# Attention in a fused transformer layer: a fifth place for k and q, loads issued in the projections' program, and value products in five places of a step

## The chip, the core and the metric

The kernel runs on one core of one Trainium2 chip. The metric is the device time of one execution in microseconds (us); less is better. The engines of a core are named as in the profile: PE is TensorE's matmul and PEld its weight load, DVE is VectorE, ACT ScalarE, POOL GpSimd and SP SyncE, which here only issues DMAs. A change of under 0.5% is taken as no change.

## The reference

One layer: attention with a window, and a mixture of experts behind it. Cut to what matters here:

```
x: (8, 512, 256)                      # 8 batches, 512 tokens, 16 heads of 16
h = layernorm(x)
Q, K, V = h @ Wq + bq, h @ Wk + bk, h @ Wv + bv
scores = Q K^T / 4 + mask             # mask: |i - j| <= 64, or i == 0, or j == 0
x = x + softmax(scores) V @ Wo + bo
x = x + experts(layernorm(x)) + shared(layernorm(x))
```

The change touches the projections Q, K, V and the attention; the output projection and the experts are as they were.

## The kernel before

**Three programs in a row.** `project`, `attend` and `mlp` each open a block of their own: every engine has its list of instructions in the block, and all engines meet at a barrier between two blocks. SP reaches the barrier behind `project` only when it has seen all its stores of q and k land (`out_s`, L217 and L218).

**The projections** go over the 8 batches. PE makes q and k of a batch, ACT and DVE split them into high and low parts in the tile `qk`, POOL copies one column (L241), and SP stores the batch's parts to the DRAM tensor `qk_parts` (L209): one DMA of 2064 KB a batch. At the start POOL clears `qs` and `ks` with three memsets (L225, L227, L229), one behind the other.

**The attention** goes over 32 steps `u`; a step is four heads of one batch (`b = u // 4`, `t = u % 4`). Its q and k lie in place `t` of `qs` and `ks`, in 96 rows: six DMAs of 129 KB bring them from `qk_parts` (`load`, L492). Each step does this:

- PE makes 16 score products into `ps_s`, a ring of three buffers (L625). DVE takes the maximum of each with the mask (L548), and then three small operations turn the 16 maxima into the tile `mt`; SP copies `mt` into two more rows of `qs` (`m_rows`, L500, four DMAs).
- PE makes the exponents in eight jobs of two products each (L643, L646; in the first two jobs also the mask, L637), into two buffers of `ps_p`. ACT takes the exponential of each (L601), and POOL clears what lies outside the window (L467).
- PE multiplies with the values: `times_v(u, i)` for four tiles `i` of keys (L673 and L679 for tile 0; L653, L657, L658 and L683 for the others). ACT takes the result out of `ps_o` (L579) and SP stores it (L504).

**The order is written out by hand.** PE runs the scores two steps ahead: in job `n` of step `u` come two scores of step `u + 2`, then the exponents of step `u`, and behind jobs 5 and 7 the value products of step `u - 1` (L691 to L699). SP issues in step `u` the maxima's rows of step `u + 1`, then, once the exponents of step `u - 1` are all made, the load of step `u + 3` into the place that step left, then the store of step `u - 2` (L521 to L528). Every fourth step DVE also takes the reciprocals of the softmax sums (L564) and SP moves them.

Names of semaphores that the text uses: `z_s` (a batch of q and k is ready to store), `qk_in` (a step's loads have landed), `mx_s` (a maximum is taken, its score buffer is free), `st_s` (a job's exponents are made), `exp_s`, `sel_s` and `nrm_s` (ACT's exponential, POOL's selection, ACT's copy out of `ps_o`).

Of the kernel before, what the change touches and what calls it, by code (L numbers as in the profile page):

```python
# [29 lines left out]
P = 128  # L30
# [16 lines left out]
HQ = 4  # L47
# [4 lines left out]
RING = 3  # L52
ZC = P + 1
# [30 lines left out]
def build(nc, d):  # L84

    with ExitStack() as ctx:
        def sem(name):
            return ctx.enter_context(nc.semaphore(name))

        def scratch(name, shape):  # L90
            return nc.dram_tensor(name, shape, F32).ap()

        d["qk"] = scratch("qk_parts", (B, 4, UB, DH, HQ, ZS))
        d["ot"] = scratch("attn_t", (B, UB, P, S))
        d["rden"] = scratch("rden", (B, NH, S))
# [16 lines left out]
        project(nc, d, sem, tally, ident, bias, eps, ks, qs, v, mask, ident16)  # L112
        attend(nc, d, sem, tally, ks, qs, v, mask, ident16)
        att.close()
        mlp(nc, d, sem, tally, ident, eps)
# [27 lines left out]
def project(nc, d, sem, tally, ident, bias, eps, ks, qs, vs, mask, ident16):  # L143
    with ExitStack() as ctx:
# [44 lines left out]
        with nc.Block() as block:  # L189
            @block.sync  # L190
            def _(sp):
# [210 lines left out]
def attend(nc, d, sem, tally, ks, qs, vs, mask, ident16):  # L402
    with ExitStack() as ctx:
# [15 lines left out]
        qk_in = [sem(f"a_qk_in{s}") for s in range(UB)]  # L419
        ones_s = sem("a_ones")  # L420
        v_s = sem("a_v")
        m_in = [sem(f"a_m_in{s}") for s in range(UB)]
# [35 lines left out]
        with nc.Block() as block:  # L458
# [28 lines left out]
            def _(sp):  # L487
                def load(u):
                    b, t = u // UB, u % UB
                    for dst, parts in ((qs, (0, 0, 1)), (ks, (2, 3, 2))):  # L490
                        for n, part in enumerate(parts):
                            sp.dma_start(dst[n * DH:(n + 1) * DH, t].bitcast(F32), d["qk"][b, part, t]).then_inc(qk_in[t], 16)  # L492

                def m_rows(u):

                    t = u % UB
# [43 lines left out]
            def _(dve):  # L540
                def maxima(u):
# [15 lines left out]
                    if u >= 2:  # L557
                        dve.wait_ge(m_in[(u - 2) % UB], ((u - 2) // UB + 1) * 16 * MROWS)
# [14 lines left out]
            def _(act):  # L573
# [7 lines left out]
                def far_rows(u):  # L581

                    t = u % UB
                    act.wait_ge(m_in[t], (u // UB + 1) * 16 * MROWS)
# [25 lines left out]
            def _(pe):  # L610
                def score(u, g):

                    b, t = u // UB, u % UB
                    j, h = SCORES[g]
                    n = u * SG + g
                    if g == 0:
                        pe.wait_ge(qk_in[t], (b + 1) * 16 * LOADS)
# [9 lines left out]
                def exponents(u, n):  # L627

                    b, t = u // UB, u % UB
# [29 lines left out]

                def times_v(u, i):  # L660

                    s = u % 2
# [7 lines left out]
                    for h in range(HQ):  # L670
                        rows, v = slice(32 * h, 32 * h + 32), vx[:, s, i, h * VW:(h + 1) * VW]
                        if i == 0:
                            pe.matmul(ps_o[rows, 0:N0], v, pt[0][:, s, h, 0:N0], start=True, stop=True, skip_group_check=True)  # L673
                        else:
                            near(rows, v, pt[i][:, s, h], i)
                    for h in range(HQ):
                        rows, v = slice(32 * h, 32 * h + 32), vx[:, s, i, h * VW:(h + 1) * VW]
                        if i == 0:
                            last = pe.matmul(ps_o[rows, N0:S], v[0:1], pt[0][0:1, s, h, N0:S], start=False, stop=True,  # L679
                                             skip_group_check=True)  # L680
                        else:
                            z = FAR[i]
                            last = pe.matmul(ps_o[rows, 0:1], v, pt[i][:, s, h, z:z + 1], start=False, stop=True,  # L683
                                             skip_group_check=True)
                    if i == NT - 1:
                        last.then_inc(av_s, 1)

# [3 lines left out]
                for u in range(NU):  # L691
                    for n in range(SJ):
# [1296 lines left out]
```

## Time and profile before

| | us |
|---|---|
| median of 3 runs | 1362.97 |
| lowest and highest | 1359.61, 1365.81 |
| the profiled execution | 1356.66 |
| its span, first to last instruction | 1354.9 |

The profiled execution is 6.3 us under the median. In its span, the projections take the first 110 us, the attention lies between 110 and 491 us, and the rest is the output projection and the experts. Times in rows are from the start of the span. A row of the timeline has the start, the duration (of a merged row from its first start to its last end), the engine, the line, the operation, what is written and read, the count, and in brackets how long the engine sat idle before it and what ended that. SPq rows are issues of DMAs, not their transfers.

### The profile page before, as it was taken

The numbers are of one execution on the slowest core, as the hardware profiler recorded it, in microseconds if no ns is written. First come the engines' busy times: TensorE is split into PE (matmuls) and PEld (weight loads), VectorE is DVE, ScalarE is ACT, GpSimd is POOL, SyncE is SP. The second block draws the span as 40 slices with busy tenths as digits, with TensorE's granted clock in tenths as the row PEclk, the third lists the DMA queues.
The fourth block names the chain that finished last, engine by engine and source line by source line (L and its number), as shares of the span: only waits on it lengthen the run. The fifth ranks groups of instructions, "written<-read, shape, count | busy, mean of one in ns | idle before, by whom it ended". The sixth has DMA issues, their size and how long they took to land. (4 is left out here: it accounts for less than half of the span.)

```text
span 1354.9 us, 23514 instructions
## 1 busy us (share of the span) xinstructions
PE 1191.9 (88%) x8906; PEld 979.6 (72%) x8906; DVE 868.0 (64%) x2246; ACT 599.0 (44%) x959; POOL 612.8 (45%) x698
## 2 busy tenths in 40 slices
PE   2995898989899833899999599999999999999997
PEld 1883665656666523798887488888888888888886
DVE  7885676766666405674788686666666666666641
ACT  1440555555555522444322255555455555454542
POOL 6000333434343324452200157667676676776654
PEclk9995899999998876789999799999999999999999
DMA  2778367566656245531012344444434444444411
GB/s 87 248 267 157 58 105 109 87 108 98 112 91 105 51 129 152 162 114 51 32 40 101 109 140 125 109 112 123 124 103 116 125 125 125 107 105 116 125 31 16
DMA packets 62094, 149.09 MB, mean 110 GB/s; under 512 B 14736, under 2 KB 31520, under 8 KB 52640
## 3 DMA queue, kind: packets, MB, share of 16 engines
q1 hardware_dynamic: 49328, 128.72, 36.3%
q0 software_dynamic: 12656, 18.90, 7.7%
q8 instruction: 69, 1.13, 0.4%
q14 instruction: 41, 0.34, 0.1%
HBM read 104.73 MB, written 42.34 MB: 109 GB/s over the span
## 5 line engine op out<-in xcount | busy, mean ns | idle before, releaser
L548 DVE CUSTOM_DVE_ANT_0 junk_s<-ps_s,mask 128x258 bf16<-128x258 f32 (+2 forms) x512 | 211.9, 472 | 123.5 <-PE ps_s L625 122.1
L601 ACT ACTIVATE pt<-ps_p 128x516 f32<-128x516 f32 (+2 forms) x256 | 167.7, 682 | 158.3 <-PE ps_p L643 94.5
L467 POOL TENSOR_SCALAR_AFFINE_SELECT pt<-pt 128x256 f32<-128x256 f32 x352 | 132.3, 415 | 230.3 <-ACT pt L601 230.3
L1775 POOL TENSOR_TENSOR h_lo<-h,h_hi 128x512 fp32r<-128x512 f32 x128 | 178.8, 1408 | 119.6 <-ACT h_hi L1811 119.3
L1885 PE MATMUL ps_gu<-xt_hi,w_hi 128*128 128x512 f32 x512 | 202.9, 396 | 2.1 <-DVE xt_lo L1834 2.1
L625 PE MATMUL ps_s<-ks,qs 96*128 96x258 f32 (+2 forms) x512 | 164.6, 380 | 45.6 <-DMA ks<-qk_parts 43.6
L1885 PE MATMUL ps_gu<-xt_lo,w_hi 128*128 128x512 f32 x512 | 200.1, 391 | 0.0
L1885 PE MATMUL ps_gu<-xt_hi,w_lo 128*128 128x512 f32 x512 | 199.9, 390 | 0.0
L1850 DVE TENSOR_TENSOR h<-ge,ps_gu 128x512 f32<-128x512 f32 x128 | 87.8, 686 | 168.2 <-ACT ge L1805 147.7
L1712 DVE TENSOR_TENSOR w_lo<-w,w_hi 128x768 fp32r<-128x768 f32 x128 | 174.1, 1364 | 31.3 <-ACT w_hi L1707 27.8
L1784 POOL DMA_INDIRECT out<-ys,idx x64 | 137.1, 2142 | 72.3 <-ACT ys L1821 57.4
L625 PEld LDWEIGHTS ps_s<-ks,qs 96*128 96x128 f32 x512 | 99.3, 207 | 87.1 <-DMA ks<-qk_parts 45.2
L1902 PE MATMUL ps_y<-w_hi,h_hi 128*128 128x256 f32 x512 | 146.4, 286 | 3.4 <-ACT ys L1821 3.4
L1902 PE MATMUL ps_y<-w_lo,h_hi 128*128 128x256 f32 x512 | 144.8, 283 | 0.0
L1902 PE MATMUL ps_y<-w_hi,h_lo 128*128 128x256 f32 x512 | 144.8, 283 | 0.0
L1805 ACT ACTIVATE ge<-ps_gu 128x512 f32<-128x512 f32 x128 | 76.2, 596 | 120.9 <-PE ps_gu L1885 120.2
L1679 POOL DMA_INDIRECT xg<-h_rows,idx x64 | 62.8, 981 | 125.4 <-DVE idx L1670 105.6
L1707 ACT ACTIVATE w_hi<-w 128x768 fp32r<-128x768 f32 x128 | 106.4, 837 | 16.9 <-PEq L852 16.9
L1885 PEld LDWEIGHTS ps_gu<-xt_hi,w_hi 128*128 128x128 f32 x512 | 96.6, 189 | 21.3 <-issue 2.5
L1885 PEld LDWEIGHTS ps_gu<-xt_hi,w_lo 128*128 128x128 f32 x512 | 96.4, 188 | 20.5
L1885 PEld LDWEIGHTS ps_gu<-xt_lo,w_hi 128*128 128x128 f32 x512 | 96.7, 189 | 18.5
L1902 PEld LDWEIGHTS ps_y<-w_hi,h_hi 128*128 128x128 f32 x512 | 98.0, 191 | 7.2 <-ACT ys L1821 6.6
(220 smaller groups left out, 2399.8 us busy)
## 6 DMA issues: line engine op xcount, KB each, us to landing
w<-in_We SPq DMA_DIRECT2D x48, 1024.0 KB, 4.9
qk_parts<-qk SPq DMA_DIRECT2D x8, 2064.0 KB, 7.7
qs<-qk_parts SPq DMA_DIRECT2D x96, 129.0 KB, 3.8
ks<-qk_parts SPq DMA_DIRECT2D x96, 129.0 KB, 5.6
x<-in_x SPq DMA_DIRECT2D x16, 512.0 KB, 8.6
attn_t<-on SPq DMA_DIRECT2D x32, 256.0 KB, 5.6
ot<-attn_t SPq DMA_DIRECT2D x32, 128.0 KB
rd<-rden SPq DMA_DIRECT2D x16, 256.0 KB
```

Of the source, the lines that this page charges most:

```text
L467: last = pool.affine_select(out=part, in_=part, pattern=[[0, HQ], [sign, WIN]], compare_op=ALU.is_ge, fill=0.0, base=sign * (n % 2) * WIN, ...
L548: dve.tensor_tensor_reduce(junk[:, (u * SG + g) % RING, 0:n], ps_s[:, (u * SG + g) % RING, 0:n], m, 1.0, -3e38, ALU.add, ALU.max, mx[:, u ...
L601: act.activation(dst, src, ACT.Exp, scale=SCALE).then_inc(exp_s, 1)
L625: pe.matmul(out, q, k, start=True, stop=True).then_inc(sc_s, 1)
L1707: act.activation(self.hi[:, s, cs], self.w32[:, cs], ACT.Copy).then_inc(self.hi_s, 1)
L1712: eng.tensor_tensor(self.lo[:, s, cs], self.w32[:, cs], self.hi[:, s, cs].bitcast(F32), ALU.subtract).then_inc(self.lo_s, 1)
L1775: pool.tensor_tensor(h_lo[:, m], h32[:, (e * KI + m) % HB], h_hi[:, m].bitcast(F32), ALU.subtract).then_inc(hlo_s, 1)
L1784: pool.indirect_dma_start(d["out"], bass.IndirectOffsetOnAxis(ap=idx[:, e % SLOTS, c:c + 1], axis=0), ys[:, e % 2, c], None, compute_op=AL ...
L1805: act.activation(ge[:, m % 2], ps_gu[:, m % 2, 0], ACT.Gelu).then_inc(gelu_s, 1)
L1850: dve.tensor_tensor(h32[:, (e * KI + m) % HB], ge[:, m % 2], ps_gu[:, m % 2, 1], ALU.mult).then_inc(h_s, 1)
L1885: last = pe.matmul(ps_gu[:, m % 2, n], l, r, start=c == 0, stop=c == 3 * KD - 1)
L1902: last = pe.matmul(ps_y[:, t % 2, 0:D], l, r, start=c == 0, stop=c == 3 * KI - 1)
```

## The change

It does five things. `qs` and `ks` get five places for steps instead of four (`SL`), and their semaphores too. The loads of the first five steps are issued in the projections' program, behind the store of the sixth batch and ahead of those of the last two; before, those of the first four steps were issued at the start of the attention's program. In the attention's steps, the load of step `u + 4` stands where that of step `u + 3` stood. The value products stand behind jobs 2, 4, 5 and 6 instead of in two groups behind jobs 5 and 7. And the far part of tile 0 is split off as `far_v`, behind job 3.

```
+SL = 5
...
-        ks = att.enter_context(nc.sbuf_tensor("ks", [P, UB, HQ, ZS], F32R))
-        qs = att.enter_context(nc.sbuf_tensor("qs", [P, UB, HQ, ZS], F32R))
+        ks = att.enter_context(nc.sbuf_tensor("ks", [P, SL, HQ, ZS], F32R))
+        qs = att.enter_context(nc.sbuf_tensor("qs", [P, SL, HQ, ZS], F32R))
...
+        qk_in = [sem(f"a_qk_in{s}") for s in range(SL)]
...
                 with sp.Fori(0, B // 2 - 1) as i:
                     step(i, 0, True)
                     step(i, 1, True)
+                sp.wait_ge(ready, 4)
+                for u in range(SL):
+                    sp.wait_ge(out_s[u // UB % 2], (u // UB // 2 + 1) * 16)
+                    load_step(sp, d, ks, qs, qk_in, u)
                 step(B // 2 - 1, 0, False)
                 step(B // 2 - 1, 1, False)
...
+def load_step(sp, d, ks, qs, qk_in, u):
+
+    for dst, parts in ((qs, (0, 0, 1)), (ks, (2, 3, 2))):
+        for n, part in enumerate(parts):
+            sp.dma_start(dst[n * DH:(n + 1) * DH, u % SL].bitcast(F32), d["qk"][u // UB, part, u % UB]).then_inc(qk_in[u % SL], 16)
...
-                for u in range(UB):
-                    load(u)
                 m_rows(0)
...
-                    if 1 <= u <= NU - UB:
+                    if 1 <= u <= NU - SL:
                         sp.wait_ge(st_s, u * SJ)
-                        load(u + UB - 1)
+                        load_step(sp, d, ks, qs, qk_in, u + SL - 1)
...
+                def far_v(u):
+
+                    for h in range(HQ):
+                        rows, v, p = parts_of(u, 0, h)
+                        pe.matmul(ps_o[rows, N0:S], v[0:1], p[0:1, N0:S], start=False, stop=True, skip_group_check=True)
...
-                        if u >= 1 and n in (5, 7):
-                            times_v(u - 1, n - 5)
-                            times_v(u - 1, n - 4)
-                for i in range(NT):
+                        if u >= 1 and n == 2:
+                            times_v(u - 1, 0)
+                        if u >= 1 and n == 3:
+                            far_v(u - 1)
+                        if u >= 1 and 4 <= n <= 6:
+                            times_v(u - 1, n - 3)
+                times_v(NU - 1, 0)
+                far_v(NU - 1)
+                for i in range(1, NT):
                     times_v(NU - 1, i)
```

SP's list between the two programs, before: the last two stores of q and k, the barrier, and then the loads of four steps.

```order
L212 COMPARE_AND_BRANCH
L209 DMA qk_parts<-qk 128x8x516 [waits p_z] x2
L189 UNCONDITIONAL_BRANCH [waits p_out1,p_out0]
L486 UNCONDITIONAL_BRANCH [waits barrier_Pool_Activation_PE_DVE_SP_release]
L492 DMA qs<-qk_parts 16x2064 x3
L492 DMA ks<-qk_parts 16x2064 x3
```

The same place now, from the end of the loop over batches (three of the four waiting pairs on `p_out0` left out):

```order
L214 COMPARE_AND_BRANCH
L412 DMA qs<-qk_parts 16x2064 [waits p_out0,p_ready]
L412 DMA qs<-qk_parts 16x2064 x2
L412 DMA ks<-qk_parts 16x2064 x3
...
L412 DMA qs<-qk_parts 16x2064 [waits p_out1]
L412 DMA qs<-qk_parts 16x2064 x2
L412 DMA ks<-qk_parts 16x2064 x3
L211 DMA qk_parts<-qk 128x8x516 [waits p_z] x2
L191 UNCONDITIONAL_BRANCH [waits p_out1,p_out0]
L498 UNCONDITIONAL_BRANCH [waits barrier_Pool_Activation_PE_DVE_SP_release]
L506 DMA qs<-mt 2x16x32 [waits a_mt]
```

The 30 loads now stand ahead of two stores for which the barrier waits, and the maxima's rows come first in the attention's program.

PE's list in the second half of a step before (`ps_s` scores, `ps_p` exponents, `ps_o` value products), from job 4:

```order
L625 MATMUL ps_s<-ks,qs 128x258 [waits a_mx] x2
L646 MATMUL ps_p<-qs,ks 128x258 [waits a_exp]
L646 MATMUL ps_p<-qs,ks 128x258
L673 MATMUL ps_o<-pt,vx 32x192 [waits a_nrm,a_v,a_exp]
L673 MATMUL ps_o<-pt,vx 32x192 x3
L679 MATMUL ps_o<-pt,vx 32x320 x4
L653 MATMUL ps_o<-pt,vx 32x256 [waits a_sel]
L653 MATMUL ps_o<-pt,vx 32x256 x3
L683 MATMUL ps_o<-pt,vx 32x1 x4
L625 MATMUL ps_s<-ks,qs 128x194 [waits a_mx] x2
```

And now, from job 2 on, as far as the first piece of tile 1:

```order
L629 MATMUL ps_s<-ks,qs 128x258 [waits a_mx] x2
L650 MATMUL ps_p<-qs,ks 128x258 [waits a_exp]
L650 MATMUL ps_p<-qs,ks 128x258
L680 MATMUL ps_o<-pt,vx 32x192 [waits a_nrm,a_v,a_exp]
L680 MATMUL ps_o<-pt,vx 32x192 x3
L629 MATMUL ps_s<-ks,qs 128x258 [waits a_mx] x2
L650 MATMUL ps_p<-qs,ks 128x258 [waits a_exp]
L650 MATMUL ps_p<-qs,ks 128x258
L695 MATMUL ps_o<-pt,vx 32x320 x4
L629 MATMUL ps_s<-ks,qs 128x258 [waits a_mx] x2
L650 MATMUL ps_p<-qs,ks 128x258 [waits a_exp]
```

Two scores and two exponents now lie between any two groups of value products.

## Rows read from the trace of the kernel before

**Rows 1.** Windows: busy time of each engine in the attention, clock, DMA share

```profile
core 0: us, PE busy (x) PEld busy (x) DVE busy (x) ACT busy (x) POOL busy (x), PEclk, DMA share, GB/s
...
137.00:488.00 351.00, 317.51 (x3422) 211.76 (x3422) 218.18 (x1053) 188.13 (x319) 142.95 (x383) 0.94 0.56 91
```

**Rows 2.** Groups of instructions by line and shape, 137 to 487.7 us: idle before, releasers

```profile
L625 PEld LDWEIGHTS ps_s<-ks,qs 96*128 96x128 f32 x478 | 89.5, 201 | 65.9 <-DVE mx L548 31.1 <-DMA ks<-qk_parts 29.1
...
L625 PE MATMUL ps_s<-ks,qs 96*128 96x512 f32 x118 | 44.8, 463 | 28.0 <-DMA ks<-qk_parts 27.7 <-DVE mx L548 0.3
...
L548 DVE CUSTOM_DVE_ANT_0 junk_s<-ps_s,mask 128x194 bf16<-128x194 f32 x120 | 35.9, 355 | 49.4 <-PE ps_s L625 49.4
```

**Rows 3.** Timeline of the start: POOL's first and last memset, DVE, PE

```profile
0.97 6.98 POOL L225 MEMSET qs<- 128x8256 f32 x1
...
7.89 15.51 DVE L299 TENSOR_SCALAR xn<-x,mv,rstd 128x256 f32<-128x256 f32 x4
...
15.04 7.00 POOL L229 MEMSET ks<- 2x8256 f32 x1
...
23.55 1.94 PE L351 MATMUL ps_t<-ident,xn 128*128 128x128 f32 x8 [23.55 <-DVE xn L299]
```

**Rows 4.** Timeline of SP's issues between the programs

```profile
84.25 18.79 SPq L209 DMA_DIRECT2D qk_parts<-qk  x3
110.31 1.29 SPq L492 DMA_DIRECT2D qs<-qk_parts  x3
...
127.79 20.57 SPq L500 DMA_DIRECT2D qs<-mt  x12
```

**Rows 5.** Windows: one store of a batch, and the loads of four steps

```profile
103.50:109.20 5.70, 0.15 (x2) 0.00 (x0) 0.69 (x1) 0.00 (x0) 0.00 (x0) 0.82 0.98 371
111.00:134.50 23.50, 14.68 (x34) 9.78 (x34) 14.00 (x68) 0.00 (x0) 0.65 (x2) 0.50 1.01 136
```

**Rows 6.** Loads of q, 110 to 140 us: time from issue to landing

```profile
DMA to landing us min/median/max: 3.2/7.7/13.2
```

**Rows 7.** Timeline of the attention's start: first score, first exponents

```profile
119.53 8.69 PE L625 MATMUL ps_s<-ks,qs 96*128 96x512 f32 x19 [15.88 <-DMA ks<-qk_parts]
...
136.76 0.21 ACT L586 ACTIVATE qs<-qs 2x8 fp32r<-2x8 f32 x1 [35.21 <-DMA qs<-mt]
...
137.03 0.50 PE L637 MATMUL ps_p<-mask,ident 128*128 128x192 bf16 x2 [1.96 <-ACT qs L586]
```

**Rows 8.** Timeline of one step of the attention without a wait for loads

```profile
342.97 0.34 PE L637 MATMUL ps_p<-mask,ident 128*128 128x192 bf16 x2
...
348.04 0.53 PE L673 MATMUL ps_o<-pt,vx 128*32 128x192 f32 x8
...
349.78 0.47 PE L625 MATMUL ps_s<-ks,qs 96*128 96x194 f32 x2
...
352.72 0.34 PE L637 MATMUL ps_p<-mask,ident 128*128 128x192 bf16 x2
```

**Rows 9.** Timeline of a step behind a long wait for loads

```profile
321.06 0.73 PE L625 MATMUL ps_s<-ks,qs 96*128 96x512 f32 x2 [2.61 <-DMA ks<-qk_parts]
...
321.63 0.34 PE L637 MATMUL ps_p<-mask,ident 128*128 128x192 bf16 x2
...
332.20 0.34 PE L637 MATMUL ps_p<-mask,ident 128*128 128x192 bf16 x2
```

**Rows 10.** Windows: PE's granted clock behind that wait

```profile
322.50:326.00 3.50, 3.50 (x14) 2.72 (x13) 2.81 (x11) 2.79 (x4) 0.00 (x0) 0.55 1.17 151
```

**Rows 11.** Timeline of PE in the last step but one, which has no scores

```profile
466.54 0.51 PE L646 MATMUL ps_p<-qs,ks 128*128 128x258 f32 x2 [0.44 <-ACT pt L601]
467.94 1.00 PE L646 MATMUL ps_p<-qs,ks 128*128 128x258 f32 x4 [0.90 <-ACT pt L601]
469.14 0.80 PE L646 MATMUL ps_p<-qs,ks 128*128 128x258 f32 x2 [0.20 <-ACT pt L601]
```

**Rows 12.** Chain of waits, 150 to 450 us: us in total, times, longest

```profile
PE ps_s L625 <- DMA ks<-qk_parts: 25.0, 15, 3.7
```

More of the change, by code:

```diff
@@ L111, in build @@
         ident16 = att.enter_context(nc.sbuf_tensor("ident16", [P, P], BF16))
-        project(nc, d, sem, tally, ident, bias, eps, ks, qs, v, mask, ident16)
-        attend(nc, d, sem, tally, ks, qs, v, mask, ident16)
+        qk_in = [sem(f"a_qk_in{s}") for s in range(SL)]
+        project(nc, d, sem, tally, ident, bias, eps, ks, qs, v, mask, ident16, qk_in)
+        attend(nc, d, sem, tally, ks, qs, v, mask, ident16, qk_in)
         att.close()
@@ L139, in mlp, with project @@
         experts(nc, d, sem, tally, ident, lists, weights)
-def project(nc, d, sem, tally, ident, bias, eps, ks, qs, vs, mask, ident16):
+def project(nc, d, sem, tally, ident, bias, eps, ks, qs, vs, mask, ident16, qk_in):
     with ExitStack() as ctx:
@@ L418, in attend @@
         ps_o = ctx.enter_context(nc.psum_tensor("ps_o", [P, S], F32))
-        qk_in = [sem(f"a_qk_in{s}") for s in range(UB)]
         ones_s = sem("a_ones")
         v_s = sem("a_v")
-        m_in = [sem(f"a_m_in{s}") for s in range(UB)]
+        m_in = [sem(f"a_m_in{s}") for s in range(SL)]
         sc_s = sem("a_sc")
@@ L487, in _ @@
             def _(sp):
[L488 to L492, printed above, removed]
                 def m_rows(u):
-                    t = u % UB
+                    t = u % SL
                     sp.wait_ge(mt_s, u + 1)
@@ L581, in far_rows @@
                 def far_rows(u):
-                    t = u % UB
-                    act.wait_ge(m_in[t], (u // UB + 1) * 16 * MROWS)
+                    t = u % SL
+                    act.wait_ge(m_in[t], (u // SL + 1) * 16 * MROWS)
                     rows = qs[M_ROW:M_ROW + 2, t]
@@ L611, in score @@
                 def score(u, g):
-                    b, t = u // UB, u % UB
+                    t = u % SL
                     j, h = SCORES[g]
@@ L616, in score @@
                     if g == 0:
-                        pe.wait_ge(qk_in[t], (b + 1) * 16 * LOADS)
+                        pe.wait_ge(qk_in[t], (u // SL + 1) * 16 * LOADS)
                     if n >= RING:
@@ L627, in exponents @@
                 def exponents(u, n):
-                    b, t = u // UB, u % UB
+                    t = u % SL
                     i, p = TJOBS[n]
@@ L658, in near, with parts_of @@
                         pe.matmul(out[:, WIN:W[i]], v, p[:, WIN + 1:W[i] + 1], start=False, stop=True, skip_group_check=True)
+                def parts_of(u, i, h):
+                    return slice(32 * h, 32 * h + 32), vx[:, u % 2, i, h * VW:(h + 1) * VW], pt[i][:, u % 2, h]
                 def times_v(u, i):
-                    s = u % 2
                     if i == 0:
@@ L670, in times_v @@
                     for h in range(HQ):
-                        rows, v = slice(32 * h, 32 * h + 32), vx[:, s, i, h * VW:(h + 1) * VW]
+                        rows, v, p = parts_of(u, i, h)
                         if i == 0:
-                            pe.matmul(ps_o[rows, 0:N0], v, pt[0][:, s, h, 0:N0], start=True, stop=True, skip_group_check=True)
+                            pe.matmul(ps_o[rows, 0:N0], v, p[:, 0:N0], start=True, stop=True, skip_group_check=True)
                         else:
[L675 to L683, printed above, removed]
+                            near(rows, v, p, i)
+                    if i > 0:
+                        for h in range(HQ):
+                            rows, v, p = parts_of(u, i, h)
+                            last = pe.matmul(ps_o[rows, 0:1], v, p[:, FAR[i]:FAR[i] + 1], start=False, stop=True,
                                              skip_group_check=True)
@@ L686, in times_v @@
                         last.then_inc(av_s, 1)
+                def far_v(u):
+                    for h in range(HQ):
+                        rows, v, p = parts_of(u, 0, h)
+                        pe.matmul(ps_o[rows, N0:S], v[0:1], p[0:1, N0:S], start=False, stop=True, skip_group_check=True)
                 for u in range(2):
```

4 lines of the change are left out of this document (2 added, 2 removed).

## The prediction

> **What bounds the kernel now.** I read the windows first, to see which engine fills each stage, then the groups of instructions by line and shape with the idle time before them, and then the timelines of the places that the change touches. Between 137 and 488 us PE is busy for 317.5 of 351 us and DVE for 218.2 [rows 1]. So PE sets the pace of the attention, and what counts is where PE stands still or goes slower than it could. Three things show. PE waits 27.7 us for loads of q and k, all ahead of a step's first score. Its weight loads wait 31.1 us for DVE to give back a score buffer, in many short pieces. And DVE waits 49.4 us ahead of the maxima of 194 columns, which come just behind a group of value products [rows 2]: PE is slowed by DVE in one part of a step and starves it in another. What stands behind the attention waits for it as a whole, so what is gained there comes off the time. The same holds for the two stretches ahead of it: PE does nothing until 23.55 us and then runs through the projections, and the attention's first score comes at 119.53 us, when loads land [rows 3, 7].
>
> **The change part by part.** All sums are made against the profiled execution, 1356.66 us, which is 6.3 us under the median of the runs.
>
> *Longer memsets: +5.0 us.* POOL clears `qs` and `ks` in three memsets, of 6.98 us for 8256 columns [rows 3]; I take the same rate for all three. With 10320 columns each takes 6.98 x 10320 / 8256 = 8.7 us, together 5.2 us more. POOL itself has time: its next need is the column copy of the first batch, late in the projections. But DVE's four short subtractions for `xn` take 15.5 us, from 7.89 to 23.4, and end 1.4 us behind the last memset, which ends at 22.04. PE's first instruction waits for them until 23.55 [rows 3]. So DVE comes through only between the memsets, and the last two subtractions come behind the third, wherever it ends. I take the end of the third memset at 27.25 and the rest as it is, a little less for one subtraction that fits in an earlier gap: 5.0 us later, for PE and for everything behind it. Bounds: 0 if the subtractions pass another way, and 5.2. The Trainium skill (SBUF — State Buffer, "Who interferes with whom") says that DVE in its two-port modes and GpSimd share a pair of ports, and that the one that comes later blocks for the other's whole instruction; by that rule this term would be 5.0 as well. The row agrees with it, and the change's cost here cannot be seen in the diff of the attention.
>
> *Loads ahead of the last two stores: +13.7 us for the first score.* SP issues the sixth store at 84.25, the eighth at the end of that row, 102.6. The eighth's transfer fills the DMA engines until 109.1, 6.5 us behind its issue and 5.5 us of full share; 1.2 us later the attention's program starts, with a first issue at 110.31 [rows 4, 5]. The 24 loads are slower: they fill the engines from 111 to 134.5 at 136 GB/s where the store has 371 [rows 5], 1.0 us for each. SP issues three of them in 1.29 us [rows 4], so a queue builds up, and the time to landing grows from 3.2 to 13.2 us [rows 6]. The maxima's rows of step 0, tiny DMAs issued from 127.79, are there only at 136.76, behind the last load [rows 4, 7]. I read this as one queue that is served in order. Now 30 loads stand behind the sixth store: from 84.25 + 6.5 = 90.7 they fill the engines for 30 us, until 120.7. SP issues them within 14 us, so the last two stores are in the queue behind them; 5.5 us each, until 131.7, and 1.2 us to the program's start: 132.9. Then all loads have landed, and PE starts its scores 0.3 us later, at 133.2 instead of 119.53. Nothing in the projections waits for these stores before the barrier. PE idles in that time, as it did before for 15.9 us [rows 7].
>
> *Rows of the maxima without a queue: -1.6 us.* From the first score to the first exponents it was 17.5 us, of which 1.96 us are PE's wait for these rows [rows 7]. With no loads ahead of them they come some 12 us behind the first score (8 us for the maxima, four issues, a landing), ahead of PE's 32nd score. I leave 0.35 us. Together the first exponents come 12.1 us later, besides the 5.0.
>
> *Loads two steps ahead: -27.8 us.* The load of step `u + 4` is issued where that of `u + 3` was, about 3 to 5 us into the step, and needed a step later. A step's six loads take 6 us, a step 9.8. What is late today, by 3.7 us at most [rows 12], has more than 9 us more. I take all 27.7 us [rows 2] and round up for the weight load in front. Bound: not less than 20, if the seven longest waits, which stand behind the reciprocals' DMAs, kept 1 us each.
>
> *The clock behind these waits: -5.3 us.* Behind a wait of 2.6 us the granted clock is down at 0.55, near the lower of its two levels (1.2 GHz), for 3.5 us [rows 10], and the step takes 10.57 us instead of 9.75 [rows 8, 9]. The timeline has seven waits of more than 2.5 us in the steps, 157 to 453 us; 0.75 us each. The Trainium skill (TensorE: Matmul & The Clock Gate, Part 1) says that idle time lets the gate close and that activity opens it again; by that rule the seven stretches go with their waits.
>
> *Value products in five places: -12.9 us.* A step without a wait takes 9.75 us [rows 8]. PE's weight loads wait 31.1 us for buffers in 31 steps, 1.0 us a step [rows 2]; that is the most this part can give back, save for a few tenths at POOL's and ACT's waits. The value products behind job 5 hold PE for 1.74 us, from 348.04 to 349.78 [rows 8], and DVE stands still ahead of the next maxima, 49.4 us in 30 steps [rows 2]. Ahead of them, jobs 2 to 5 go at DVE's pace. With a piece of 0.5 to 0.7 us behind each of the jobs 2 to 6, PE has work of its own there while DVE empties the ring, and DVE never sees a pause longer than three buffers cover. What stays is the lag of the first two jobs, whose four maxima of 512 columns are DVE's longest, and a new one: DVE now finishes a step's small operations while PE is already in the next. Of 1.0 us a step I take 0.55 (the waits behind jobs 0 and 1 and half of one other stay): 16.5 us in 30 steps. In seven steps DVE also has the reciprocals, 0.5 us, so far done in its idle time; that shows now: 3.6 back. Bounds: 0 and 31.
>
> *The last two steps: -3 us.* They have no scores, and PE waits for ACT 0.44 + 0.90 + 0.20 = 1.54 us in one [rows 11], as much in the other. The pieces fill these waits.
>
> The other edits cost nothing by themselves: as many matmuls, the same DMAs for each step. One step's load less in the attention, one more ahead.
>
> Sum: +5.0 + 13.7 - 1.6 - 27.8 - 5.3 - 12.9 - 3.0 = -31.9 us. 1356.7 - 31.9 = 1324.8 in the profiled execution's terms; with the 6.3 us to the median, **1331 us**.
>
> **The rivals.**
>
> 1. *The stores pass the loads, or the loads go faster beside them: 1312 us.* For it: the store moves 371 GB/s with the same engines full [rows 5], so the loads are held up by something that a store beside them may not need. If 30 loads of 0.132 MB went at 371 GB/s they would take 10.7 us, the stores would end at 90.7 + 10.7 + 11 = 112.4, and the first score would come at 113.9, 5.6 us earlier than before instead of 13.7 later: 19.3 less. Against it: the landing times grow as in a queue served in order [rows 6]. The Trainium skill (DMA: Bandwidth & Descriptors, "Two DMAs through the same engine are not ordered") says that descriptors of one queue start in order but are pipelined; by that rule something of this kind is possible. Chance 0.15.
> 2. *The value products give nothing: 1347 us.* The waits for DVE turn into others, for ACT's exponentials (its eight, with the copy out of `ps_o` between the first two, hold up job 3) or for the maxima's rows in the step behind the reciprocals. Then 12.9 and 3.0 fall away. For it: DVE's work is unchanged, and each of the waits is short. Against it: DVE is busy for only 218 of 351 us. Chance 0.18.
> 3. *The loads still come late: 1364 us.* If the wait is for something else than issue time, such as the exponents of the step before, the 27.8 and 5.3 stay. Against it: the place is left by the same step, one place further on. Chance 0.06.
> 4. *Each border between value products and scores costs PE time: slower.* Other weights, of 32 columns instead of 128, other rows of `ps_o`; three more borders in each of 31 steps. At the two borders of today the next score starts where the products end [rows 8], so I see no price. From rival 2's time it takes 0.25 us a border to pass 1370; at 0.35 it would be 1347 + 93 x 0.35 = 1380 us. Chance 0.05.
>
> **How the numbers follow.** My forecast has 0.56, with a range of its own from 1318 to 1342. Rivals 1 and 2 lie on its two sides, 1312 and 1347; a range from 1306 to 1348 takes in most of them and leaves out rivals 3 and 4 and the tails. 0.5% of the median is 6.8 us, about what a measurement of this kernel can tell from no change. Faster by more: forecast, rivals 1 and 2, 0.88 with the tails cut. Within 0.5%: rival 3 and a tail, 0.07. Slower: 0.05.
>
> **What would show it.** PE's first instruction at 28.5 us. Thirty issues of loads between 89 and 104 us, and two stores that land more than 20 us behind their issue; the attention's first issue near 138 us. No wait for loads in the steps, and a granted clock of 1.0 there. Steps of 9.1 us, 9.7 in every fourth, and DVE's idle time ahead of the maxima of 194 columns nearly gone. If instead the first score comes before 125 us, the queue is not what I take it for, and if steps still take 9.75 us, another wait took the place of DVE's.

## The result, and the profile after

| | before | after |
|---|---|---|
| median, us | 1363.37 | 1339.67 |
| lowest and highest of 4 | 1359.61, 1365.81 | 1338.48, 1340.61 |
| the profiled execution | 1356.66 | 1340.61 |

The ratio is 0.9828, with a 95% interval from 0.9804 to 0.9852: faster by 23.7 us, where I had forecast 32. The time lies 8.7 us above the forecast and inside the range. Medians here and below are of all executions, the ratios and their intervals of the fast ones alone: one execution of before beside runs 1 to 4, of 6147.78 us, is in the median and not in the ratios. Below, the rows of after that answer to those shown of before; the same code has somewhat higher line numbers there.

The timeline of the start:

```profile
0.98 8.70 POOL L231 MEMSET qs<- 128x10320 f32 x1
7.79 20.48 DVE L305 TENSOR_SCALAR xn<-x,mv,rstd 128x256 f32<-128x256 f32 x4
...
18.51 8.72 POOL L235 MEMSET ks<- 2x10320 f32 x1
...
28.42 1.94 PE L357 MATMUL ps_t<-ident,xn 128*128 128x128 f32 x8 [28.42 <-DVE xn L305]
```

The memsets are longer in proportion to their columns, and PE's first instruction is 4.87 us later than in [rows 3].

SP's issues between the programs, then PE and ACT at the start of the attention:

```profile
90.33 2.81 SPq L412 DMA_DIRECT2D qs<-qk_parts  x3
...
105.73 1.34 SPq L412 DMA_DIRECT2D ks<-qk_parts  x3
107.11 10.19 SPq L211 DMA_DIRECT2D qk_parts<-qk  x2
...
140.04 8.65 PE L629 MATMUL ps_s<-ks,qs 96*128 96x512 f32 x19 [31.12 <-PEq L191]
...
152.34 0.21 ACT L590 ACTIVATE qs<-qs 2x8 fp32r<-2x8 f32 x1 [45.52 <-DMA qs<-mt]
...
155.35 0.55 PE L641 MATMUL ps_p<-mask,ident 128*128 128x192 bf16 x2
```

The windows of the loads, of the two stores behind them, and of the attention without its ends (columns as in [rows 1]):

```profile
96.50:127.00 30.50, 12.42 (x82) 11.03 (x80) 8.66 (x12) 4.47 (x6) 0.48 (x2) 0.78 1.04 133
127.50:138.90 11.40, 0.00 (x0) 0.00 (x0) 0.00 (x0) 0.00 (x0) 0.00 (x0) 0.50 1.03 365
155.00:460.00 305.00, 294.99 (x3290) 197.23 (x3288) 225.46 (x1060) 189.34 (x313) 141.15 (x373) 0.99 0.62 101
```

First 133 GB/s, then 365, each at full share: the two stores move only when the loads are through. The first score comes 20.5 us later than in [rows 7]. PE's releaser there is its own sequencer at the program's start, where it was a DMA: the loads have long landed, and the barrier sets the time. The first exponents come 18.3 us later. Then PE is busy for 295 of 305 us, in before for 276.

The list of waits between 150 and 470 us has no wait of PE for loads left. What PE itself waits for DVE is this (columns as in [rows 12]):

```profile
PE ps_s L629 <- DVE mx L552: 6.2, 13, 0.8
```

The waits for score buffers did not shrink as forecast. The same groups as in [rows 2], from 155 to 470 us:

```profile
L552 DVE CUSTOM_DVE_ANT_0 junk_s<-ps_s,mask 128x258 bf16<-128x258 f32 x240 | 92.6, 424 | 37.1 <-PE ps_s L629 36.9
L629 PEld LDWEIGHTS ps_s<-ks,qs 96*128 96x128 f32 x478 | 78.7, 189 | 62.4 <-DVE mx L552 58.1
...
L552 DVE CUSTOM_DVE_ANT_0 junk_s<-ps_s,mask 128x194 bf16<-128x194 f32 x120 | 38.3, 358 | 28.1 <-PE ps_s L629 28.1
```

The weight loads are idle for 58.1 us where they had 31.1. DVE's idle time ahead of the maxima of 194 columns fell from 49.4 to 28.1 us, and 36.9 us stand ahead of those of 258 columns, where there were 4.5.

And one step on PE, 9.67 us from one first mask product to the next:

```profile
329.65 0.34 PE L641 MATMUL ps_p<-mask,ident 128*128 128x192 bf16 x2
...
332.31 0.41 PE L650 MATMUL ps_p<-qs,ks 128*128 128x258 f32 x2
332.65 0.53 PE L680 MATMUL ps_o<-pt,vx 128*32 128x192 f32 x8
333.11 0.51 PE L629 MATMUL ps_s<-ks,qs 96*128 96x258 f32 x2
333.45 0.40 PE L650 MATMUL ps_p<-qs,ks 128*128 128x258 f32 x2
333.79 0.74 PE L695 MATMUL ps_o<-pt,vx 1*32 1x320 f32 x8
...
339.32 0.34 PE L641 MATMUL ps_p<-mask,ident 128*128 128x192 bf16 x2
```

9.67 is hardly less than the 9.75 of [rows 8], where 9.1 was forecast. That is the miss. A merged row's duration overlaps the next row, so the pace is read from start to start: behind the value products, the two scores take 333.45 - 333.11 = 0.34 us, and the two exponents ahead of the next group again 0.34. Beside them, PE in the same kind of job of before, where no value products are near:

```profile
346.66 0.41 PE L625 MATMUL ps_s<-ks,qs 96*128 96x258 f32 x2
346.91 0.41 PE L646 MATMUL ps_p<-qs,ks 128*128 128x258 f32 x2
347.16 0.70 PE L625 MATMUL ps_s<-ks,qs 96*128 96x258 f32 x2
347.70 0.41 PE L646 MATMUL ps_p<-qs,ks 128*128 128x258 f32 x2
```

There scores and exponents take 0.25 us each, and only the pair ahead of the group at 348.04 [rows 8] takes 0.34. So a border has a price, about 0.09 us on each side, and I had looked for it in the wrong place: in a gap behind the products, where it lies in the pace of the pairs beside them. Three more groups have six more sides, some 0.5 us a step. That is a reading; runs 2, 8, 10 and 11 try it. (A group of value products has two sides: the pair of exponents ahead of it and the pair of scores behind it. The prediction counts one border for each group.)

### The profile page after: what moved, and what is told of

Read it like the earlier page. It is cut to its first block and busy times, and to the rows that moved or that the text cites. A ratio compares the mean times of both kernels' runs of the same rounds, so it can differ in the third digit from the quotient of the medians.

```text
span 1338.9 us, 23515 instructions
## 1 busy us (share of the span) xinstructions
PE 1179.9 (88%) x8906; PEld 973.1 (73%) x8906; DVE 878.6 (66%) x2246; ACT 604.2 (45%) x959; POOL 620.3 (46%) x698
## 5 line engine op out<-in xcount | busy, mean ns | idle before, releaser
L552 DVE CUSTOM_DVE_ANT_0 junk_s<-ps_s,mask 128x258 bf16<-128x258 f32 (+2 forms) x512 | 217.1, 472 | 97.1 <-PE ps_s L629 96.8
L1789 POOL TENSOR_TENSOR h_lo<-h,h_hi 128x512 fp32r<-128x512 f32 x128 | 178.8, 1408 | 120.9 <-ACT h_hi L1825 120.7
L605 ACT ACTIVATE pt<-ps_p 128x516 f32<-128x516 f32 (+2 forms) x256 | 170.5, 680 | 117.2 <-PE ps_p L650 83.0
L1726 DVE TENSOR_TENSOR w_lo<-w,w_hi 128x768 fp32r<-128x768 f32 x128 | 173.9, 1362 | 31.2 <-ACT w_hi L1721 27.8
L629 PE MATMUL ps_s<-ks,qs 96*128 96x258 f32 (+2 forms) x512 | 157.0, 376 | 39.9 <-PEq L191 31.1
L629 PEld LDWEIGHTS ps_s<-ks,qs 96*128 96x128 f32 x512 | 88.5, 195 | 98.8 <-DVE mx L552 61.6
```

The costliest lines, as they stand in the source:

```text
L552: dve.tensor_tensor_reduce(junk[:, (u * SG + g) % RING, 0:n], ps_s[:, (u * SG + g) % RING, 0:n], m, 1.0, -3e38, ALU.add, ALU.max, mx[:, u ...
L605: act.activation(dst, src, ACT.Exp, scale=SCALE).then_inc(exp_s, 1)
L629: pe.matmul(out, q, k, start=True, stop=True).then_inc(sc_s, 1)
L1726: eng.tensor_tensor(self.lo[:, s, cs], self.w32[:, cs], self.hi[:, s, cs].bitcast(F32), ALU.subtract).then_inc(self.lo_s, 1)
L1789: pool.tensor_tensor(h_lo[:, m], h32[:, (e * KI + m) % HB], h_hi[:, m].bitcast(F32), ALU.subtract).then_inc(hlo_s, 1)
```

## The experiments

Each time stands with the ratio to before and its 95% interval. The medians of before were 1362.18 us beside runs 1 to 4, 1359.81 beside 5 and 6, 1360.51 beside 7 to 9 and 1362.33 beside 10 to 12.

**1. Five places, nothing else.** Before, with room for a fifth place.

```
+SL = 5
-        ks = att.enter_context(nc.sbuf_tensor("ks", [P, UB, HQ, ZS], F32R))
+        ks = att.enter_context(nc.sbuf_tensor("ks", [P, SL, HQ, ZS], F32R))
```

> The kernel before with the two tiles made for five places and cleared whole; only four are used, everything else is as before. Theory (DVE's subtractions get through only between POOL's memsets, so the ends of the memsets set when PE starts): PE's first instruction moves from 23.55 to 28.4 us and the time goes up by 5 us, 1363 to 1368. Rival (the shift is absorbed by waits in the projections): PE's start moves, the time stays at 1363. Rival (the fifth place costs by its mere addresses in the attention): steps of the attention get longer.

Measured: 1364.96 us, 1.0038 [1.0009, 1.0066]. In its timeline the first score is 5.7 us later than in [rows 7]:

```profile
7.81 20.47 DVE L300 TENSOR_SCALAR xn<-x,mv,rstd 128x256 f32<-128x256 f32 x4
...
125.20 8.69 PE L626 MATMUL ps_s<-ks,qs 96*128 96x512 f32 x19 [16.34 <-DMA ks<-qk_parts]
```

So the later start is real, and it comes with the size of two tiles that nobody reads in that stretch. In the whole time it is a rise of 0.38%, as expected in size, but by itself less than what is taken as a change here.

**2. Value products in two groups.** After, with the groups where before had them.

```
-                        if u >= 1 and n == 2:
-                            times_v(u - 1, 0)
...
+                        if u >= 1 and n == 5:
+                            times_v(u - 1, 0)
+                            far_v(u - 1)
+                            times_v(u - 1, 1)
+                        if u >= 1 and n == 7:
+                            times_v(u - 1, 2)
+                            times_v(u - 1, 3)
```

> The changed kernel with the value products back in two groups behind jobs 5 and 7; five places and early loads stay. Theory (each border between value products and scores costs PE some 0.15 us, which takes back nearly all that the waits for DVE gave): steps of 9.75 us, 2 to 5 us above the changed kernel's 1340, 1342 to 1345. Rival (the prediction's size: five groups are worth 16 us): 1356. Rival (five groups cost more than they give): below 1340.

Measured: 1341.71 us, 0.9843 [0.9801, 0.9885]. That is 2.0 us above after's median, and the two intervals overlap, where the terms of -12.9 and -3.0 made 16.

The rows show where the gain went. Here every step from 2 to 28 takes 9.73 to 9.76 us, the steps with the reciprocals too. In after the commonest step is 9.67 us, but those with the reciprocals take 10.04 to 10.32, and five others 9.92 to 9.94. The mean of the 27 steps is 9.82 us in after (9.79 to 9.80 in runs 3, 4 and 7, whose steps have the same instructions) and 9.74 here: in the steps with scores, five groups cost 0.05 to 0.08 us. In four of the five others, as in two with the reciprocals, one of DVE's small operations takes 0.43 us instead of 0.17. It starts together with one of POOL's or 0.01 us behind it:

```profile
339.44 1.15 POOL L479 TENSOR_SCALAR_AFFINE_SELECT pt<-pt 128x256 f32<-128x256 f32 x3 [0.74 <-ACT pt L605]
339.45 0.43 DVE L558 SCALAR_TENSOR_TENSOR nm<-mx,nm 128x16 fp32r<-128x16 f32 x1
```

That is after; in this run the operation takes 0.17 or 0.18 us in all of these steps. What five groups give lies in the end of the attention, from the first mask product of step 29 to the last value product. First this run, then after:

```profile
435.95:472.73 36.78, 33.25 (x363) 19.45 (x362) 7.71 (x36) 17.73 (x30) 13.75 (x37) 0.75 0.10 33
438.24:468.52 30.28, 27.26 (x363) 16.84 (x362) 8.87 (x39) 18.22 (x31) 14.73 (x39) 0.95 0.12 40
```

The 6.5 us are not the groups' alone. The granted clock differs, 0.75 against 0.95, and it does so between executions of the same instructions too: this stretch takes 32.92 us at a clock of 0.83 in run 4 and 28.88 at 1.00 in run 3.

**3. The stores first.** After, with the 30 loads behind the last two stores.

```
-                sp.wait_ge(ready, 4)
-                for u in range(SL):
...
                 step(B // 2 - 1, 0, False)
                 step(B // 2 - 1, 1, False)
+                sp.wait_ge(ready, 4)
+                for u in range(SL):
...
```

> The changed kernel with the 30 loads issued behind the last two stores of q and k, still in the projections' program. Theory (one queue served in order): the stores land some 7 us behind their issue; SP reaches the barrier when it has issued the loads, near 122 us, first score at 122.5 instead of 140.0; but the maxima's rows now stand behind the loads, which end near 144.5, so the first exponents come at 147 instead of 155.4: 8.5 us less than the changed kernel, 1331. Rival (the stores were held up by something else than the loads ahead of them): first score stays near 140, 1340.

Measured: 1330.95 us, 0.9765 [0.9724, 0.9807]. Its timeline:

```profile
97.80 9.68 SPq L211 DMA_DIRECT2D qk_parts<-qk  x2
107.59 2.97 SPq L412 DMA_DIRECT2D qs<-qk_parts  x3
...
125.02 8.66 PE L629 MATMUL ps_s<-ks,qs 96*128 96x512 f32 x19 [16.94 <-PEq L191]
```

The first score is 15 us earlier than in after, the first exponents (147.81) 7.5 us: the maxima's rows now stand behind 30 loads and reach ACT at 147.54. The first exponents and the time are as expected (147 and 1331), the first score is 2.5 us later. Loads and stores were moved in order of issue here, as in after: the queue is served in order.

**4. Small memsets.** After, with each memset cut into 20 of 516 columns.

```
+                for tile, rows, value in ((qs, slice(0, P), 0.0), (ks, slice(0, P), 0.0), (ks, slice(M_ROW, M_ROW + 2), 1.0)):
+                    for s in range(SL):
+                        for h in range(HQ):
+                            pool.memset(tile[rows, s, h].bitcast(F32), value).then_inc(ready, 1)
```

> The changed kernel with each memset of the two tiles cut into twenty of 516 columns. Theory (a subtraction of DVE waits for the end of the memset that POOL is in, and gets through between two): each of the four waits at most 0.5 us, they end near 11 us instead of 28.3, PE's first instruction at 11 to 13 us, and 15 us of the time go: 1325. Rival (DVE gets through only when POOL has done all it has queued): PE starts at 29 to 32 us, 1340 to 1344.

Measured: 1325.88 us, 0.9731 [0.9689, 0.9773]. The start of its timeline:

```profile
0.98 9.44 POOL L235 MEMSET qs<- 128x516 f32 x20
7.85 4.56 DVE L306 TENSOR_SCALAR xn<-x,mv,rstd 128x256 f32<-128x256 f32 x4
10.48 19.91 POOL L235 MEMSET ks<- 128x516 f32 x40
```

The four subtractions take 4.56 us instead of 20.48, and PE starts at 12.55. The memsets end later than in after, at 30.4 instead of 27.2, and it does no harm: DVE was never waiting for their result, only for a gap between them. Four such subtractions with no memset beside them take 1.38 us (before, at 30.02 us), so the holdup fell from 19.1 us to 3.2. The Trainium skill (SBUF — State Buffer, "Who interferes with whom") says that DVE in its two-port modes and GpSimd share a pair of ports, and that the later one is blocked for the other's whole instruction. The run agrees, as far as the times go: with instructions a twentieth as long, most of the holdup goes. In which mode DVE ran no row shows.

**5. Five groups alone.** Before, with its four places and its loads, and the value products as in after.

```
-                        if u >= 1 and n in (5, 7):
-                            times_v(u - 1, n - 5)
-                            times_v(u - 1, n - 4)
+                        if u >= 1 and n == 2:
+                            times_v(u - 1, 0)
...
```

> The kernel before with the value products in five places, and nothing else of the change: four places, loads in the attention's program. Theory (borders take back what the waits for DVE give): steps without a wait for loads shrink from 9.75 to 9.66 us, PE's wait for loads stays near 28 us, 2 to 5 us less than before, 1359 to 1361. Rival (the prediction's size): 1347. Rival (borders cost more than the waits gave): above 1363.

Measured: 1381.92 us, 1.0185 [1.0144, 1.0226]: slower, where I expected no change. The timeline on PE, and the window behind its wait:

```profile
343.48 1.22 PE L625 MATMUL ps_s<-ks,qs 96*128 96x512 f32 x2 [2.16 <-DMA ks<-qk_parts]
...
355.85 0.34 PE L637 MATMUL ps_p<-mask,ident 128*128 128x192 bf16 x2
...
367.28 1.22 PE L625 MATMUL ps_s<-ks,qs 96*128 96x512 f32 x2 [2.23 <-DMA ks<-qk_parts]
```

```profile
344.00:348.50 4.50, 4.50 (x15) 3.08 (x14) 2.81 (x9) 1.92 (x3) 0.00 (x0) 0.50 0.66 113
```

The waits for loads sum to about what they were in before (29.8 us on PE against 27.7 in [rows 2]), but lie otherwise: some 2.2 us in every second step. Behind all but the first two of them the granted clock is at its lower level (0.50 is 1.2 GHz) for 4.5 us or more. In before only the seven long waits, of 2.6 to 3.7 us, had a low clock behind them; 155 to 460 us has a mean clock of 0.87 here, 0.95 in before. The steps take 11.4 and 12.4 us in turn.

**6. Three groups.** Tile 0 behind job 3, tiles 1 and 2 behind job 5, tile 3 behind job 6.

```
+                        if u >= 1 and n == 3:
+                            times_v(u - 1, 0)
+                            far_v(u - 1)
+                        if u >= 1 and n == 5:
+                            times_v(u - 1, 1)
+                            times_v(u - 1, 2)
+                        if u >= 1 and n == 6:
+                            times_v(u - 1, 3)
```

> The changed kernel with the same value products in three groups, behind jobs 3 (tile 0, near and far), 5 (tiles 1 and 2) and 6 (tile 3). Theory (two borders fewer a step, 0.15 to 0.25 us each, and no group longer than 1.15 us, so that three score buffers still cover most of DVE): steps of 9.3 to 9.4 us, 8 to 10 us less than the changed kernel, 1331. Rival (a border is free and the length of a group counts): 9.7 us or more, 1340 or above.

Measured: 1349.52 us, 0.9933 [0.9913, 0.9953], with steps of 9.95 us. It is slower than two groups and than five, so my expectation fell. Two rows of DVE in one step:

```profile
339.45 0.43 DVE L552 CUSTOM_DVE_ANT_0 junk_s<-ps_s,mask 128x258 bf16<-128x258 f32 x1 [1.12 <-PE ps_s L629]
...
342.00 0.36 DVE L552 CUSTOM_DVE_ANT_0 junk_s<-ps_s,mask 128x194 bf16<-128x194 f32 x1 [1.07 <-PE ps_s L629]
```

Each group of 1.1 us leaves DVE idle for as long. That alone does not say why three are the slowest. In such a step DVE waits 2.68 us here in three pieces, 2.46 in run 2 in two (the longer of 1.71), and 2.22 in after in five. The run also differs from run 2 in a second thing: it has no group behind job 7, and by run 11 a group there is worth more than 0.2 us a step. No run separates the two.

**7. All the cures at the front.** Small memsets; the load of step 0 between the last two stores, those of steps 1 and 2 behind them, those of steps 3 and 4 in the attention, behind the maxima's rows.

```
+                sp.wait_ge(out_s[0], 16)
+                load_step(sp, d, ks, qs, qk_in, 0)
                 step(B // 2 - 1, 1, False)
+                for u in range(1, 3):
+                    load_step(sp, d, ks, qs, qk_in, u)
...
                 m_rows(0)
+                load_step(sp, d, ks, qs, qk_in, 3)
```

> The changed kernel with the small memsets, and with the loads spread: step 0 between the last two stores of q and k, steps 1 and 2 behind the last store, steps 3 and 4 in the attention's program behind the maxima's rows of steps 0 and 1. Theory (queue in order; the DMA engines have a gap of some 4 us between two stores, and SP needs 0.46 us an issue): the barrier opens as soon as the last store has landed, first score some 25 us earlier than in the changed kernel, first exponents 16 us behind it, and 15 us from the memsets: 40 us less than 1340, 1300. Rival (the gains overlap, since the projections get longer when their start is no longer held back): 1310 or above.

Measured: 1300.45 us, 0.9552 [0.9528, 0.9577]. Its timeline at the start of the attention:

```profile
103.46 8.66 PE L635 MATMUL ps_s<-ks,qs 96*128 96x512 f32 x19 [8.64 <-PEq L191]
...
118.78 0.54 PE L647 MATMUL ps_p<-mask,ident 128*128 128x192 bf16 x2
```

The first exponents are 36.6 us earlier than in after, and the time is 39.2 us less. What the change costs at the front can be had back, and more: the time to the first exponents doesn't need the loads of the later steps.

**8. A sixth group.** After, with tile 3's four products of one column behind job 7.

```
+                        if u >= 1 and n == 7:
+                            far_column(u - 1, NT - 1)
```

> The changed kernel with the four one-column products of tile 3's far key moved from the group behind job 6 to a sixth group behind job 7: no work added, one border more on either side. Theory (a border holds up the next weight load, 0.1 us on either side): steps of 9.8 to 9.85 us instead of 9.66, 1344 to 1346. Rival (borders are free, the step is set by DVE alone): 9.66 us, 1340.

Measured: 1336.0 us, 0.9843 [0.98, 0.9885], steps of 9.63 to 9.65. I had expected two more sides to cost. They didn't, and the mean of steps 2 to 28 is 9.73 us against after's 9.82: behind job 7 comes the place where PE waits for DVE anyway, and that wait is 0.37 us here where after has 0.58.

**9. Four places.** After, with `SL = 4`: the loads are a step less ahead.

```
-SL = 5
+SL = 4
```

> The changed kernel with the number of places set to four: the loads of the first four steps early, the load of step u + 3 in step u, value products in five places. Theory (with five groups a late load is followed each time by a stretch at the lower clock, so the two parts of the change need each other): waits for loads in every second step, 28 us, steps of 11.4 and 12.4 us in turn, up to 56 us more in the steps and 11 less ahead of them: 1380 to 1385. Rival (issuing the first loads early is what the change lives on): 1340 or less.

Measured: 1387.51 us, 1.0203 [1.0179, 1.0226]. One row of its chain of waits:

```profile
PE ps_s L629 <- DMA ks<-qk_parts: 30.7, 15, 2.5
```

The waits are back, every second step, with the clock at 0.88, as in run 5; the time is 2.5 us above the upper end of what I expected. The early loads are still there, so it is the fifth place that removes the waits. The value products' places depend on it: five groups with four places are slower than before, here and in run 5.

**10. More borders, same order of work.** After, with the one-column products of tiles 1 and 2 moved one job on, between its scores and its exponents.

```
                             score(u + 2, 2 * n + 1)
+                        if u >= 1 and n in (5, 6):
+                            far_column(u - 1, n - 4)
                         exponents(u, n)
```

> The changed kernel with the one-column products of tiles 1 and 2 cut off from their groups and put one job later, between the scores and the exponents of jobs 5 and 6, where the trace shows no wait of PE for DVE. No work is added, four borders between value products and others more in each step. Theory (a border costs PE 0.1 us on either side where nothing hides it): steps of 10.0 to 10.05 us instead of 9.66, 1350 to 1352. Rival (borders are free; the sixth group cost nothing for that reason): 9.66 us, 1340.

Measured: 1358.72 us, 0.9967 [0.9944, 0.9991], steps of 10.29 to 10.33 where none has the reciprocals: nearly twice the lengthening that I expected. PE in one of the two jobs, up to the scores of the other:

```profile
335.97 0.64 PE L657 MATMUL ps_o<-pt,vx 128*32 128x256 f32 x8
336.54 0.50 PE L629 MATMUL ps_s<-ks,qs 96*128 96x258 f32 x2
336.98 0.24 PE L689 MATMUL ps_o<-pt,vx 128*32 128x1 f32 x8
337.15 0.51 PE L650 MATMUL ps_p<-qs,ks 128*128 128x258 f32 x2
337.58 0.64 PE L657 MATMUL ps_o<-pt,vx 128*32 128x256 f32 x8
338.15 0.47 PE L629 MATMUL ps_s<-ks,qs 96*128 96x194 f32 x2
```

The weight load of the last row, and DVE's last record ahead of it:

```profile
338.15 0.30 PEld L629 LDWEIGHTS ps_s<-ks,qs 96*128 96x128 f32 x2 [0.41 <-DVE mx L552]
```

```profile
337.66 0.08 DVE L552 DVE_READ_ACCUMULATOR2_ANT mx<- 128x1 f32 x1
```

From start to start: scores 0.44 us with a border on both sides (0.34 with one, 0.25 with none), exponents 0.43, and the eight products ahead of scores 0.57, in both jobs, where they had 0.45 ahead of the one-column products. A job like this is 0.33 us longer, two are the 0.65 us of the step. The weight load's idle time is put down to DVE, but DVE had its last maximum by 337.74, 0.41 us before the scores start, and was itself waiting: the named releaser had long been done. So borders cost PE time by themselves in the jobs that go at PE's pace: 0.09 us on a side of a pair, or 0.16 if the whole 0.65 us is put on the four new sides.

**11. The last group later.** After, with the groups behind jobs 2, 3, 4, 5 and 7.

```
-                        if u >= 1 and 4 <= n <= 6:
+                        if u >= 1 and n in (4, 5):
                             times_v(u - 1, n - 3)
+                        if u >= 1 and n == 7:
+                            times_v(u - 1, 3)
```

> The changed kernel with the value products behind jobs 2, 3, 4, 5 and 7 instead of 2 to 6. Theory (jobs 2 to 6 run at PE's own pace, jobs 7, 0 and 1 at DVE's, so work moved into job 7 is hidden; the sixth group was free for that reason): the 0.5 us of tile 3 and a border or two leave PE's part, steps of 9.1 to 9.3 us instead of 9.66, 1325 to 1330. Rival (the step is one loop of PE, DVE and ACT, and only its sum counts): 9.66 us, 1340.

Measured: 1330.87 us, 0.9753 [0.9718, 0.9789], with as many borders as after and steps of 9.44 to 9.50, those with the reciprocals too:

```profile
334.89 0.34 PE L641 MATMUL ps_p<-mask,ident 128*128 128x192 bf16 x2
...
344.34 0.34 PE L641 MATMUL ps_p<-mask,ident 128*128 128x192 bf16 x2
```

In after, PE runs ahead in jobs 3 to 6 and then waits for DVE in the last job and the first two, where DVE has its small operations and its longest maxima. The last group belongs there. The direction was as expected, the size a little less. The steps with the reciprocals no longer stand out, so the mean of steps 2 to 28 is 9.46 us against 9.82, 0.36 less.

**12. Run 7 with run 11.** Both edits together.

> Small memsets and spread loads, 1300 us, together with the value products behind jobs 2, 3, 4, 5 and 7. Theory (both gains are independent, in different stages): as much under 1300 as the last-group-later kernel is under 1340, 1285 to 1290. Rival: 1300.

Measured: 1293.05 us, 0.9485 [0.9449, 0.9521], steps of 9.45 us. It is the fastest version, 46.6 us under after's median, and 3 us above the upper end of what I expected.

## Why the prediction was right, and where it was off

**Longer memsets, +5.0.** Right: 4.87 at PE's first instruction, 5.7 at the first score in run 1. The cause, that DVE gets through only between memsets, is shown by run 4.

**Loads ahead of the stores, +13.7.** Right in kind, too small by 1.8 us together with the memsets: the first score is 20.5 us later with the memsets' part, where the terms made 18.7. The loads' transfers still fill the engines at 127 us, where I had them end at 120.7 plus the 5 of the memsets. Rival 1, that stores and loads overlap, is out: 133 GB/s and then 365, and run 3.

**The maxima's rows, -1.6.** Seen: no wait ahead of the first exponents. From first score to first exponents it is 15.3 us, 2.2 less than before, where 1.6 was forecast.

**Waits for loads, -27.8, and their clock, -5.3.** Right. The exponents and value products, from the first exponents to the last value product, take 350.9 us in before, 317.6 in run 2 and 313.2 in after. Run 2 has the five places and not the five groups, and its 33.3 us less stand against 33.1 in the two terms. 27.7 of them are waits [rows 2], and the mean clock from 155 to 460 us went from 0.95 in before to 0.99 in after. Rival 3 is out, and run 9 shows which part does it.

**Value products in five places, -12.9, and the last two steps, -3.0.** Here is the miss. The step behind it is the one in rival 4 that says "At the two borders of today the next score starts where the products end, so I see no price". By the rows the part gave 4.4 us where 15.9 stood (317.6 in run 2, 313.2 in after), by the medians 2.0. None of it comes from the steps that the term of -12.9 was about: from the first exponents to step 29 after takes 282.9 us and run 2 280.8, and the end of the attention is 6.5 us shorter, in part by the clock. The time is rival 2's for this part, the mechanism rival 4's, at a price of some 0.09 us a side, 0.18 a border, and not 0.35. In the common step the gain that I had taken, 0.55 us, and six sides at 0.09 all but cancel; what is left is 0.08, and the longer steps of after turn it round.

Three more sentences of the reasoning fail. "DVE never sees a pause longer than three buffers cover": in the step shown above DVE stands idle five times, for 0.20 to 0.56 us, and its idle time for scores in all, 65.6 us, is about run 2's (68.4, from 155 to 468.5 us). The 31.1 us of the weight loads' waits were not "the most this part can give back": run 2 has 36.7 us of them with steps of 9.74, run 11 43.2 with 9.46, and by run 10 some that are put down to DVE are none of its. And I let only "the waits behind jobs 0 and 1" stay, while by run 11 the last job is DVE's too, and a group there is worth 0.2 us in the common step and 0.36 in the mean. The steps with the reciprocals, +0.4 each where I had 0.5, came as forecast, two of the six from step 2 to 28 at +0.65.

**The sum.** In the profiled execution's terms the forecast was 1324.8, and after's profile has 1340.61: 15.8 us more. The value products and the last two steps are 11.5 of it, the loads and memsets 1.8, and 3.4 lie behind the attention, in a program that the change leaves as it was (870.4 us against 867.0); the maxima's rows gave 0.6 back. Between the medians the miss is only 8.7 us, because before's profiled execution was 6.3 us under its median and after's 0.9 above. That the time came as near as it did is in part luck.

**What stays open.** Why a border costs time: the rows show longer pairs, not what holds them up. The weight loads of a pair beside a group start with it rather than ahead of it, which would fit, and no run separates it. Why nearly all the waits of 2.2 us in run 5 bring the clock down, and before's of 0.9 didn't, was not tried. Nor was why DVE's small operation is longer beside POOL's in some steps of after, and why the end of the attention gets another clock from one execution to the next.

## What to carry to other kernels

Work moved into another engine's waiting time can pay a price at each border with other weights: here 0.09 us a side, in the jobs that go at PE's pace. Read it from start to start of the neighbours' rows, and count sides before spreading work out. Put the pieces where the waits are, in the jobs that go at the other engine's pace, and no others. A tile made larger, or a load made earlier, can also hold up what shares its port or its queue: look for that first, since here two such side effects held back the first score by 20.5 us.

## What the hardware showed that I had not expected

Edits whose gains I had taken as additive are not. Five groups alone are 1.85% slower, and with a fifth place they are at best 2 us faster than two: without it the waits for loads, which were seven long ones and some short, lie at 2.2 us in every second step, and nearly all are followed by 4.5 us or more at half clock.

Three groups are slower than two and than five. DVE stood idle for 1.1 us behind a group of 1.1 us, and for 0.20 to 0.56 us behind pieces of 0.5 to 0.7: three buffers bridge neither wholly. Why three come out last is not shown.

The commonest step is not the mean step. Five groups shorten the first by 0.08 us and lengthen the second by as much.

The 129 KB loads into 16 rows move 133 GB/s with all engines at full share, where the stores of 128 rows move 365 behind them in the same queue. So a load's time is to be taken from its like, not from another's rate.
